# Two of four dt·u products per half moved from VectorE to GpSimd in an attention + Mamba kernel

## The reference

```
dt = softplus(einsum(dt_r, dt_proj_w) + dt_proj_b)
A = -exp(A_log)
def step(h, inp):
    dt_t, B_t, C_t, u_t = inp
    dA = exp(dt_t[:, :, None] * A)
    h = h * dA + (dt_t * u_t)[:, :, None] * B_t[:, None, :]
    y = einsum('bdn,bn->bd', h, C_t)
```

## Time and profile before

| | us |
|---|---|
| median of 3 runs | 6651.12 |
| lowest, highest | 6645.4, 6661.98 |
| the profiled execution, its time | 6657.9 |
| the profiled execution, its span | 6656.1 |
| DVE busy | 5764.2 (87%) |
| PE busy | 6107.0 (92%) |
| ACT busy | 4572.1 (69%) |
| POOL busy | 3029.0 (46%) |

### The profile page before, as it was taken

How to read it: one execution, slowest core, us unless ns; L and a number is a source line. 1 busy time by engine, 2 the same in 40 slices (tenths; PEclk the granted TensorE clock), 3 DMA queues, 4 the chain that set the end, 5 groups by cost and what they waited for, 6 DMA issues and landing times.

```text
span 6656.1 us, 114602 instructions
## 1 busy us (share of the span) xinstructions
PE 6107.0 (92%) x43104; PEld 3974.5 (60%) x43104; DVE 5764.2 (87%) x7083; ACT 4572.1 (69%) x6560; POOL 3029.0 (46%) x1538
## 2 busy tenths in 40 slices
PE   6998999989999889989899899998999988999877
PEld 2774558645585556845577455774558645685554
DVE  0787999789996999969999799988999789996995
ACT  2775678667785677847778467865778667785663
POOL 0104881068701785019830388205871068601883
PEclk8999999999999999999999999999999999999966
DMA  3535885367833678247863488535784367823664
GB/s 144 173 93 162 205 204 152 113 173 199 240 98 137 170 205 225 83 142 184 222 186 96 142 209 204 161 108 159 197 217 131 127 170 200 237 75 142 175 148 128
DMA packets 326517, 1087.52 MB, mean 163 GB/s; under 512 B 49944, under 2 KB 50072, under 8 KB 286960
## 3 DMA queue, kind: packets, MB, share of 16 engines
q1 hardware_dynamic: 245728, 656.81, 30.7%
q0 software_dynamic: 61840, 390.09, 26.1%
q10 hardware_dynamic: 18432, 33.56, 1.5%
HBM read 570.16 MB, written 241.71 MB: 122 GB/s over the span
## 4 chain that ended last, share of the span: by engine, by line
PE 61%; DVE 21%; issue 5%; DMA 5%; POOL 3%; ACT 3%; SPq 1%; DVEq 0%; ACTq 0%; POOLq 0%
PE ps L1251 33%; PE ps L1359 13%; DVE area_h L1172 13%; PE ps L1511 8%; DVE area_acc L1182 4%; PE ps L1300 3%; POOL area_s L693 2%; DMA area_s<-z_keep 2%; DMA yg_keep<-area_s 2%; PE ps L1302 1%; POOL area_s L681 1%; DVE area_dt L1160 1%; PE ps L1272 1%; DVE area_h L1139 1%; DVE area_h L1133 1%
## 5 line engine op out<-in xcount | busy, mean ns | idle before, releaser
L693 POOL TENSOR_TENSOR area_s<-area_u,area_s 128x1024 f32<-128x1024 f32 x1024 | 2493.7, 2449 | 586.1 <-DVE area_u L1163 352.5
L1172 DVE TENSOR_TENSOR_SCAN area_h<-ps,area_s 128x1024 f32<-128x1024 f32 x1024 | 2331.1, 2277 | 18.1 <-POOL area_s L693 16.8
L1511 PEld LDWEIGHTS ps<-ident,area_h 128*128 128x128 f32 x8192 | 984.1, 150 | 776.3 <-DVE area_acc L1182 431.5
L1511 PE MATMUL ps<-ident,area_h 128*128 128x128 f32 x8192 | 1192.0, 293 | 206.6 <-DVE area_acc L1182 141.7
L814 ACT ACTIVATE area_s<-area_s,negmax 128x1024 f32<-128x1024 f32 x1024 | 1179.1, 1152 | 250.4 <-DVE negmax L1068 241.9
L1068 DVE CUSTOM_DVE_ANT_0 area_s<-ps,area_dt 128x1024 f32<-128x1024 f32 x1024 | 1242.0, 1214 | 102.9 <-PE ps L1251 102.4
L892 ACT ACTIVATE ps<-area_dt,negA 128x1024 f32<-128x1024 f32 x1024 | 1146.2, 1119 | 238.6 <-DVE area_h L1172 100.6
L681 POOL TENSOR_TENSOR area_s<-area_s 128x1024 f32<-128x1024 f32 x64 | 155.9, 2437 | 2371.1 <-ACT area_s L867 2371.1
L876 ACT ACTIVATE area_w<-ps,C_nat 128x512 f32<-128x512 f32 x1024 | 703.7, 687 | 688.9 <-PE ps L1511 681.4
L1359 PE MATMUL ps<-ident,area_s 128*128 128x128 f32 x8192 | 1062.7, 273 | 0.4
L1359 PEld LDWEIGHTS ps<-ident,area_s 128*128 128x128 f32 x8192 | 955.7, 141 | 139.3 <-issue 5.4
(11 more groups left out here) (124 smaller groups left out, 5308.5 us busy)
## 6 DMA issues: line engine op xcount, KB each, us to landing
area_acc<-area_w POOLq DMA_DIRECT2D x256, 1024.0 KB, 7.6
area_s<-b_rows SPq DMA_DIRECT2D x256, 512.0 KB, 4.3
q_stack<-qk_keep SPq DMA_DIRECT2D x512, 128.0 KB, 2.8
k_stack<-qk_keep SPq DMA_DIRECT2D x512, 128.0 KB, 3.1
area_s<-z_keep SPq DMA_DIRECT2D x72, 512.0 KB, 5.3
qk_keep<-q_stack SPq DMA_DIRECT2D x128, 256.0 KB, 4.5
qk_keep<-k_stack SPq DMA_DIRECT2D x128, 256.0 KB, 4.8
y_keep<-area_acc POOLq DMA_DIRECT2D x8, 4096.0 KB, 14.8
```

Of the source, the lines that this page charges most:

```text
L693: pool.tensor_tensor(dbu[:, dl % 2, :], U[:, k // (NS * DL) * DL + dl, :], bb[:, q, :], ALU.mult).then_inc(s_dbu.sem, 1)
L1172: v.tensor_tensor_scan(out=hs[:, q, dl, :], data0=banks(2 * (dl % 2)), data1=dbu[:, dl % 2, :], initial=0.0, op0=ALU.mult, op1=ALU.add).th ...
L1511: last = nc.tensor.transpose(ps[:, 4 + n % 2, dl * P:(dl + 1) * P], hs[:, r % 2, dl, n * P:(n + 1) * P], ident[:, :])
```

## The change

The in-place products of dt and u for tiles 2 and 3 (first half) and 6 and 7 (second half) leave DVE. POOL makes them, each just ahead of the inject of the same tile in the first row of the half, after waiting for `s_dt`. The signal `s_du` is still counted up once for each product, now from either engine. In all, 4 products for each of 8 sequences move, 32 of 64.

```diff
+                def times_dt(n):
+                    pool.wait_ge(*s_dt.at(b, n + 1))
+                    pool.tensor_tensor(U[:, n, :], U[:, n, :], dT[:, n % DL, :], ALU.mult).then_inc(s_du.sem, 1)
+
                 def inject(r, dl):
                     k = r * DL + dl
                     q = r % 2
+                    if r % NS == 0 and dl >= DL // 2:
+                        times_dt(r // NS * DL + dl)
                     pool.wait_ge(*s_du.at(b, k // (NS * DL) * DL + dl + 1))
...
-                    dve.wait_ge(*s_dt.at(b, n + 1))
-                    v.tensor_tensor(U[:, n, :], U[:, n, :], dT[:, n % DL, :], ALU.mult).then_inc(s_du.sem, 1)
+                    if n % DL < DL // 2:
+                        dve.wait_ge(*s_dt.at(b, n + 1))
+                        v.tensor_tensor(U[:, n, :], U[:, n, :], dT[:, n % DL, :], ALU.mult).then_inc(s_du.sem, 1)
```

## The result

The changed kernel has a median of 6661.71 us over 20 runs (6648.75 to 6673.27); the kernel before, run beside it, has 6650.5 us over 20 runs (6644.41 to 6661.98). The ratio is 1.0018 with a 95% interval of 1.0011 to 1.0024, that is +12 us (+7 to +16): slower, but by less than 0.3%.

The account below looks back on a forecast made before the run. It took the start of scan 3 in each half, set by POOL's chain, as the bound. 8 × 1.65 + 8 × 0.33 = 15.8 us moved the median from 6651.1 to 6667 us, range 6652 to 6684.

Parts of the forecast that it names:

- What bounds: At each half's start, when scan 3 of the first row starts counts; PE and DVE have hardly any slack behind it.
- The case in which it is swallowed: Rival: the first half's late start meets a wait set elsewhere, only second halves count; 2.6 us, 6654 us, chance 0.08.
- POOL's product: Each moved product on POOL, two per half, takes 2.34 us like the inject; ends 2.32 and 2.44.
- The wait of POOL for its own product: Before each inject behind its product, POOL idles 0.25 us for that product's signal; ends 0 and 0.30.
- if the inject starts right behind its product: Sign on POOL that the forecast is wrong: no wait between a product and its inject, where 0.25 us was taken.
- First half: POOL's product, inject, product, inject behind the dt of tile 2 make scan 3 1.65 us late; ends 1.05 and 2.06.
- Second half: The same POOL chain behind the dt of tile 6 makes scan 3 0.33 us late; ends 0.10 early, 0.74 late.
- The sum: Over eight first and eight second halves, 8 × 1.65 + 8 × 0.33 = 15.8 us; ends 7.6 and 22.4.
- The cold PE: Rival: PE's longer pause keeps one more step at 1.2 GHz, 2.5 us per first half, 20 us, 6687 us; chance 0.10.
- The full difference: Rival: all 32 moved products stand on the path, each 1.12 us longer, 36 us in all, 6687 us; chance 0.05.
- DVE as the bound: Rival: DVE's own time is the limit, so the 39 us freed count in full, 6612 us; chance 0.05.
- Contention: Slowing of DVE or POOL by running beside each other at the halves' starts, priced at zero.

Follow-up runs that it names:

- e2: Changed kernel with only the products of tiles 6 and 7 on POOL, tiles 2 and 3 back on DVE; 6649.27 us, ratio 1.0004 to the kernel before.
- e5: Kernel before, plus 16 transposes of the identity filling PE's pause in each first half; 6643.14 us, ratio 0.9995.
- e6: Changed kernel, plus 26 transposes of the identity filling PE's pause in each first half; 6648.98 us, ratio 1.0003 to the kernel before.
- e1: Changed kernel with only the products of tiles 2 and 3 on POOL, tiles 6 and 7 back on DVE; 6660.02 us, ratio 1.0024 to the kernel before.
- e4: Changed kernel with only the products of tiles 3 and 7 on POOL, tiles 2 and 6 back on DVE; 6672.84 us, ratio 1.0038 to the kernel before.
- e3: Changed kernel with only the products of tiles 2 and 6 on POOL, tiles 3 and 7 back on DVE; 6641.48 us, ratio 0.9996 to the kernel before.
- e8: Changed kernel with only the products of tiles 1 and 6 on POOL, the others on DVE; 6643.02 us, ratio 0.9990 to the kernel before.

## Why the prediction was right

The range (6652 to 6684) held the measured 6661.7, the likeliest case (within 0.3%) came, and the sign of the shift was the one worked out.

- *What bounds.* Right: the end of the stretch, scan 3, is the place, and what is late there stays late. In the traces the shift is constant from the fifth accumulation to the last one of a first half (2.38 us in b = 0, 0.94 in b = 1). The case in which it is swallowed did not come.
- *POOL's product.* 2.34 us taken from the inject; L688 took 2.337 to 2.405 us, median 2.346. Right.
- *The wait of POOL for its own product.* Taken as 0.25 us, measured as 0.08. This is the term that was mis-sized. The rows that I took it from the earlier trace rows were a select behind a memset and a DMA issue behind a product, not a product behind a product. Twice 0.17 us for each half make nearly all of the difference: 9.70 us for the chain instead of 10.07. The prediction named "if the inject starts right behind its product" as a sign of being wrong, and with 0.08 us this sign came close to being met; the low end of its range (a wait of 0) had priced it.
- *First half.* 1.65 us forecast, 1.27 measured. Scan 2 was to wait some 1.8 us for POOL: it waited 1.59 us here, but 0.30 in the second half, where the dt of tile 7 comes later. The high end of 2.06 us starts POOL at 605.75, 0.21 us behind the dt of tile 2, for which no row is named; with the 0.10 us of the sum it is 1.95.
- *Second half.* 0.33 us forecast, 0.00 measured; e2 gives 1.0004. The summed +3.0 us of these halves in the trace do not arise at the start but, in single sequences, by −0.3 to +1.2 us between the sixth and the eleventh accumulation of DVE; in the trace before, POOL waits there for a load of `du_keep`. That this load makes the difference is not shown.
- *The sum.* 15.8 us forecast; with the right wait it is 8 × 1.27 = 10.2, and with PE's clock 12. Measured were +12 (+7 to +16). PE's clock, which the sum had at zero, made up for part of the waits that were too long; that the total comes within 4 us is in part luck, the sign and the place are not.
- *The cold PE.* Right as a mechanism, shown by e5 and e6, but with some 2 us in all instead of 20, so its case did not come. Counted from PE's first transposes, the granted clock rose after 3.5 to 5.0 us before the change, and after it at 5.6 or 5.7 us in four sequences and at 2.7 to 3.5 in the other four. In the four late ones the first transposes took 1.97 us as before, the products 3.62 instead of 2.7 to 3.5, and the next transposes up to 1.32 instead of 1.04: parts of a step were lost, not a whole one.
- *The full difference, and DVE as the bound.* Both out, by e1 to e4: per half the moved products cost 1.27 us (2 and 3), nothing (6 and 7) or 1.18 (3 or 7 alone), and gained 1.25 (6 alone), depending on what ran beside them.
- *Contention.* Priced at zero, and rightly for this change, because DVE keeps only the products of tiles 0, 1, 4 and 5; they took 1.22 to 1.65 us as before. The row of 1.63 us was read as a rough fit to a lock (0.41 us more for 0.55 us of overlap); it was an exact one, since it ended 1.08 us behind POOL's end like all others. It was this pricing, kept in mind as harmless, that made me miss the first half of e3.

## What to carry to other kernels

Moving an instruction from a busy engine to an idle one helps only if the chain that passes through it becomes shorter; cost the chain from the last common event to the next thing that someone waits for, with the slower engine's duration, and not the busy shares. Move the product behind which the first engine has other work on the same chain, not the last one: tiles 3 and 7 cost 1.2 us each, tile 6 gained 1.25, and tiles 6 and 7 together gave nothing. Before splitting products with two SBUF inputs between VectorE and GpSimd, look whether two of them will run at the same time. And where DVE gets ahead, look at every engine that it waits for: in e8 it was PE's projection, whose length hung on the granted clock.

## What I had not expected

- A DVE product with two SBUF inputs that starts beside a POOL one ends 1.08 us behind POOL's end, however long the overlap (241 cases; 2.53 us instead of 1.23 in e3), while scans and dt sums with one input in PSUM lost nothing. So the split of these products bought nothing in e3's first halves.
- A GpSimd instruction that waits for its own engine's last product starts 0.08 us after its end, while a DMA issue behind such a product started 0.30 us after it.
- Sixteen transposes of no use on PE in a pause of 4 us shorten each first half by 0.1 to 1.0 us (e5), since the granted clock is up when the work comes.
